# Stage one with two sets of part buffers, turned copies read in source order, and scalings on ScalarE

## What is computed

```python
n = layernorm(x)
q, k, v = split_heads(n @ Wq + bq), split_heads(n @ Wk + bk), split_heads(n @ Wv + bv)
scores = einsum('bhid,bhjd->bhij', q, k)
rel = einsum('bhid,pd->bhip', q, rel_key)
bias = take_along_axis(rel, clip(j - i + p - 1, 0, p - 1), axis=3)
attn = softmax(where(j <= i, (scores + bias) * scale, -inf))
x = x + layernorm(merge_heads(attn @ v) @ Wo + bo)
h = silu(lin(layernorm(x), w1, s1)) * lin(layernorm(x), w2, s2)
h = gelu(lin(h, h1, sh1))
h = gelu(lin(h, h2, sh2))
x = x + layernorm(lin(h, w3, s3))
```

## Time and profile before

| | us |
|---|---|
| median of 3 runs | 740.18 (736.39 to 741.16) |
| the profiled execution | 739.48 |
| its span | 737.4 |
| PE busy | 644.0 (87%) |
| ACT busy | 572.1 (78%) |
| DVE busy | 540.2 (73%) |
| POOL busy | 247.7 (34%) |
| PE on the chain that ended last | 53% |

### The profile page before, as it was taken

The page is one execution under the profiler, slowest core; times in us unless marked ns, Lnnn a source line. Parts: engine busy times, 40 slices in busy tenths (PEclk is TensorE's granted clock), DMA queues, the critical chain, the costliest instruction groups (busy, mean ns, idle before and its releaser), DMA issues.

```text
span 737.4 us, 18944 instructions
## 1 busy us (share of the span) xinstructions
PE 644.0 (87%) x8066; PEld 467.7 (63%) x8066; DVE 540.2 (73%) x923; ACT 572.1 (78%) x660; POOL 247.7 (34%) x175
## 2 busy tenths in 40 slices
PE   4877569999999999999999999978799898998993
PEld 2433336676766766857667667655588687786682
DVE  5894787788687877786878777775677668588546
ACT  2784977988989889889898798786577868677573
POOL 2100180370640913706409128000271441731901
PEclk9988767999999999999999999997999999999997
DMA  7487424152241231521412314050300000000001
GB/s 229 110 224 225 133 63 111 35 132 66 50 114 36 73 94 35 128 70 50 106 46 70 96 34 116 24 166 2 100 1 1 0 1 1 1 29 0 5 25 59
DMA packets 39175, 52.82 MB, mean 72 GB/s; under 512 B 5656, under 2 KB 29640, under 8 KB 36680
## 3 DMA queue, kind: packets, MB, share of 16 engines
q1 hardware_dynamic: 39088, 51.58, 25.6%
HBM read 39.00 MB, written 11.81 MB: 69 GB/s over the span
## 4 chain that ended last, share of the span: by engine, by line
PE 53%; DVE 13%; ACT 12%; issue 5%; POOL 2%; DVEq 0%; ACTq 0%; POOLq 0%
PE p_o L1112 16%; PE p_s L1087 13%; PE p_z L1786 8%; PE p_z L1789 8%; DVE probs L1213 6%; ACT probs L1330 6%; PE p_s L1021 5%; POOL hid_lo L1707 1%; DVE res L1967 1%; ACT hid_hi L1890 1%; ACT o_acc L1339 1%; ACT even_b L1034 1%; ACT odd_b L1034 1%; PE p_o L1124 1%; DVE hid_lo L1991 1%
## 5 line engine op out<-in xcount | busy, mean ns | idle before, releaser
L1087 PE MATMUL p_s<-q_sb,k_sb 96*128 96x128 bf16 (+1 forms) x1600 | 172.1, 250 | 9.9 <-ACT probs L1330 4.7
L1330 ACT ACTIVATE probs<-p_s 128x1024 f32<-128x1024 f32 x160 | 156.7, 1017 | 19.9 <-DVE p_s L1222 10.8
L1112 PE MATMUL p_o<-probs,v_sb 128*32 128x128 f32 (+1 forms) x3200 | 159.9, 331 | 7.5 <-ACT o_acc L1339 4.4
L990 POOL TENSOR_SCALAR_AFFINE_SELECT even_b<-even_b 128x2048 f32<-128x2048 f32 x31 | 75.0, 2420 | 261.3 <-ACT even_b L1034 261.3
L1330 ACT ACTIVATE probs<-probs 128x1024 f32<-128x1024 f32 x128 | 133.5, 1055 | 35.7 <-DVE probs L1213 35.4
L1087 PEld LDWEIGHTS p_s<-q_sb,k_sb 96*128 96x128 bf16 x1600 | 113.8, 100 | 69.5 <-issue 29.5
L1213 DVE TENSOR_TENSOR probs<-p_s,even_b 128x1024 f32<-128x1024 f32 x96 | 114.9, 1219 | 16.6 <-PE p_s L1087 16.6
L1112 PEld LDWEIGHTS p_o<-probs,v_sb 128*32 128x32 f32 x3200 | 84.6, 111 | 41.0 <-issue 14.1
L1786 PE MATMUL p_z<-hid_hi,h_hi 128*128 128x512 f32 x256 | 102.0, 399 | 1.7 <-POOL hid_lo L1707 1.7
L1021 PE MATMUL p_s<-q_rows,rel_w 72*128 72x64 bf16 x2048 | 84.5, 197 | 20.1 <-DVE probs L1213 8.7
L1789 PE MATMUL p_z<-hid_lo,h_hi 128*128 128x512 f32 x256 | 100.9, 394 | 0.0
(11 more groups left out here) (182 smaller groups left out, 844.7 us busy)
## 6 DMA issues: line engine op xcount, KB each, us to landing
k_sb<-k_dram SPq DMA_DIRECT2D x48, 192.0 KB
q_sb<-q_dram SPq DMA_DIRECT2D x16, 576.0 KB
q_rows<-qr_dram SPq DMA_DIRECT2D x42, 192.0 KB
q_dram<-q_parts SPq DMA_DIRECT2D x12, 256.0 KB, 3.1
k_dram<-k_parts SPq DMA_DIRECT2D x12, 256.0 KB, 3.2
qr_dram<-q_turned SPq DMA_DIRECT2D x12, 256.0 KB, 3.4
x_all<-in_L_attn_x_dram SPq DMA_DIRECT2D x4, 512.0 KB, 4.2
every<-in_L_ffn_h_w_dram SPq DMA_DIRECT2D x2, 1024.0 KB, 8.4
```

Of the source, the lines that this page charges most:

```text
L990: nc.gpsimd.affine_select(out=far, in_=near, compare_op=ALU.is_ge, fill=0.0, base=-1 - r, pattern=[[0, QB], [-1, MCH * RCH]], channel_mult ...
L1087: last = nc.tensor.matmul(slot[:, c:c + n * BLK], k_sb[hg][:, h * S + j * BLK:h * S + (j + 1) * BLK], ap(q_sb[hg], at, [[HG * S, KROWS], [ ...
L1112: last = nc.tensor.matmul(p_o[32 * h:32 * h + 32, at:at + blocks * BLK], v_sb[hg][:, j, h * 32:(h + 1) * 32], probs[n % PBUFS][:, h, col * ...
L1330: nc.scalar.activation(to, got, ACT.Exp, scale=SCALE).then_inc(t_exp, 1)
```

## The change

- **Two sets.** `q_parts`, `k_parts` and `q_turned` exist twice, batch b uses set b % 2, and each semaphore of stores exists twice. ScalarE waits, from batch 2 on, for the stores of batch b-2 (`stored`). `m_parts` of batches 0 and 1 lies in `x_all`, over tokens of the same batch that are no longer needed; batches 2 and 3 have one new buffer, `m_late`, and ScalarE waits for the first m store on it before it writes batch 3's. The room comes out of `stored_room`, an unused tile. Waits at the end of stage one and in stage two are adjusted to the sets; before the first copy into `even_b`, ScalarE now waits for the m stores of batches 0 and 1.
- **Turned copies.** The same permutation is walked in the order of the source: reads go through 128 neighbouring columns, writes step over eight columns (16 bytes).
- **Scalings.** For batches 1 to 3 the eight scalings of the layer norm are ScalarE's (`scaled`), with scale and bias as pointers: those of batch 1 behind `root(1)`, those of b+2 behind `m_parts` of batch b. VectorE ends a layer norm with `nmr`.
- **Loads.** SP loads `k_sb` and `q_sb` of the second half in batch 2 instead of batch 1.
- **Bound.** The wait for `own` moves behind the first two products of each batch.

```diff
-STORED_ROOM = 5184
+STORED_ROOM = 576
+    def m_parts(b):
+
+        if b >= 2:
+            return m_late[:, :, :]
+        return x_all[0:H, b * S:(b + 1) * S].bitcast(BF16).rearrange("h (m s) -> h m s", m=MPARTS)
     def turned_view(to, part):
 
-        return to[:, part, :].rearrange("p (r i) -> p r i", i=NB)
+        return to[:, part, :].rearrange("p (r i) -> p i r", i=NB)
+
+    def stored(eng, b, sems):
+
+        for done in sems:
+            eng.wait_ge(done[b % 2], (b // 2 + 1) * (16 * PARTS))
 
     def untouched_view(got, part):
 
-        return got[:, part, :].rearrange("p (i r) -> p r i", i=NB)
+        return got[:, part, :].rearrange("p (i r) -> p i r", i=NB)
...
             if b == 2:
-                sp.wait_ge(s_mst, 16)
+                sp.wait_ge(s_mst[0], 16)
                 for hg in range(2):
                     load_m(0, hg)
             if not first:
                 shift(b - 1)
             if b == 1:
-                for done in (s_qst, s_kst, s_rst):
-                    sp.wait_ge(done, 16 * PARTS)
+                stored(sp, 0, (s_qst, s_kst, s_rst))
                 sp.dma_start(q_rows[:, :], ap(qr_dram, 0, [[DROW, PARTS * HD], [0, PARTS], [1, UH * S]])).then_inc(t_qr[0], 16)
-                for hg in range(2):
-                    load_k(0, hg)
-                    load_q(0, hg)
+            if b in (1, 2):
+                load_k(0, b - 1)
+                load_q(0, b - 1)
...
             dve.wait_ge(s_std, b + 1)
+            if not first:
+                dve.wait_ge(s_xh, b)
             nc.vector.reciprocal(rstd[:, :], std[:, :]).then_inc(s_ln, 1)
             dve.wait_ge(s_ln, b * LNS + 4)
             nc.vector.scalar_tensor_tensor(out=nmr[:, :], in0=mv[:, :, 0], scalar=-1.0, in1=rstd[:, :],
                                            op0=ALU.mult, op1=ALU.mult).then_inc(s_ln, 1)
+            if not first:
+                return
             dve.wait_ge(s_ln, b * LNS + 5)
-            if not first:
-                dve.wait_ge(s_tr, b * 2)
...
+        def scaled(b):
+            act.wait_ge(s_xin, b * 16 + 16)
+            act.wait_ge(s_ln, b * LNS + 5)
+            act.wait_ge(s_tr, b * 2)
+            for t in range(NB):
+                last = nc.scalar.activation(xh[:, t, :], x_all[:, b * S + t * E:b * S + (t + 1) * E], ACT.Identity,
+                                            scale=rstd[:, t:t + 1], bias=nmr[:, t:t + 1])
+            last.then_inc(s_xh, 1)
...
             if first:
                 root(1)
+                scaled(1)
...
             if last_batch:
+                act.wait_ge(s_mst[0], 16 * 2)
                 for c in range(FIRST_BEFORE):
                     copy_act(act, "even", c)
 
-            if not first:
-                act.wait_ge(s_turned, b * PARTS)
-                act.wait_ge(s_qst, b * (16 * PARTS))
-                act.wait_ge(s_kst, b * (16 * PARTS))
-            nc.scalar.activation(q_parts[:, 0, :], qf[:, :], ACT.Identity).then_inc(s_hi, 1)
+            if b >= 2:
+                act.wait_ge(s_turned, (b - 1) * PARTS)
+                stored(act, b - 2, (s_qst, s_kst))
+            nc.scalar.activation(q_parts[b % 2][:, 0, :], qf[:, :], ACT.Identity).then_inc(s_hi, 1)
...
+            if b + 2 < B:
+                scaled(b + 2)
             if not last_batch:
                 turn_query(b, 2)
...
             pe.wait_ge(s_pos, b + 1)
-            pe.wait_ge(s_own, b + 1)
             for j in range(2):
...
+                if j == 0:
+                    pe.wait_ge(s_own, b + 1)
```

More of the change, by code:

```diff
@@ L249, in build @@
     far_keep, near_cap = (sb(n, [128, MCH * RCH], F32, one) for n in ("far_keep", "near_cap"))
+    early_parts = [sb(f"{n}0", [128, PARTS, S], BF16, one) for n in ("q_parts", "k_parts", "q_turned")]
     sb("stored_room", [128, STORED_ROOM], F32, one)
     exp_warm = sb("exp_warm", [128, 1], F32, one)
-    q_parts, k_parts = (sb(n, [128, PARTS, S], BF16, one) for n in ("q_parts", "k_parts"))
-    m_parts = sb("m_parts", [H, MPARTS, S], BF16, one)
-    q_turned = sb("q_turned", [128, PARTS, S], BF16, one)
+    q_late, k_late = (sb(f"{n}1", [128, PARTS, S], BF16, one) for n in ("q_parts", "k_parts"))
+    m_late = sb("m_late", [H, MPARTS, S], BF16, one)
+    turned_late = sb("q_turned1", [128, PARTS, S], BF16, one)
+    q_parts, k_parts, q_turned = zip(early_parts, (q_late, k_late, turned_late))
+    def m_parts(b):
+        if b >= 2:
+            return m_late[:, :, :]
+        return x_all[0:H, b * S:(b + 1) * S].bitcast(BF16).rearrange("h (m s) -> h m s", m=MPARTS)
     pone = ExitStack()
@@ L284, in build @@
     s_turned = sem("s_turned")
-    s_rst = sem("s_rst")
+    s_rst = [sem(f"s_rst{p}") for p in range(2)]
     s_pos = sem("s_pos")
@@ L295, in build @@
     s_wabs, s_wany = sem("s_wabs"), sem("s_wany")
-    s_qst, s_kst, s_mst = sem("s_qst"), sem("s_kst"), sem("s_mst")
+    s_qst, s_kst, s_mst = ([sem(f"{n}{p}") for p in range(2)] for n in ("s_qst", "s_kst", "s_mst"))
     t_q = [sem(f"t_q{p}") for p in range(2)]
@@ L427, in sync_one @@
             turned(B - 1, part)
[L428 to L431, removed]
+        for b in (B - 2, B - 1):
+            stored(sp, b, (s_qst, s_kst, s_rst))
+        for p in range(2):
+            sp.wait_ge(s_mst[p], 16 * 2)
         sp.wait_ge(s_gap, B + 3)
@@ L510, in shift_rest @@
             dve.wait_ge(s_mneg, b * 2 + 2)
-            nc.vector.scalar_tensor_tensor(out=m_parts[:, 1, :], in0=p_tr[0:H, :], scalar=-1.0, in1=m_parts[:, 0, :],
+            nc.vector.scalar_tensor_tensor(out=m_parts(b)[:, 1, :], in0=p_tr[0:H, :], scalar=-1.0, in1=m_parts(b)[:, 0, :],
                                            op0=ALU.mult, op1=ALU.subtract).then_inc(s_mr, 1)
@@ L560, in batch @@
             dve.wait_ge(s_hi, b * 2 + 1)
-            nc.vector.tensor_tensor(q_rest[:, :], qf[:, :], q_parts[:, 0, :], ALU.subtract).then_inc(s_rest, 1)
+            nc.vector.tensor_tensor(q_rest[:, :], qf[:, :], q_parts[b % 2][:, 0, :], ALU.subtract).then_inc(s_rest, 1)
             dve.wait_ge(s_hi, b * 2 + 2)
-            nc.vector.tensor_tensor(k_rest[:, :], kf[:, :], k_parts[:, 0, :], ALU.subtract).then_inc(s_rest, 1)
+            nc.vector.tensor_tensor(k_rest[:, :], kf[:, :], k_parts[b % 2][:, 0, :], ALU.subtract).then_inc(s_rest, 1)
             if not last_batch:
@@ L649, in turn_query @@
             act.wait_ge((s_hi, s_mid, s_low)[part], b * 2 + 1)
-            if b > 0 and part == 0:
-                act.wait_ge(s_rst, 16 * PARTS * b)
-            nc.scalar.activation(turned_view(q_turned, part), untouched_view(q_parts, part),
+            if b >= 2 and part == 0:
+                stored(act, b - 2, (s_rst,))
+            nc.scalar.activation(turned_view(q_turned[b % 2], part), untouched_view(q_parts[b % 2], part),
                                  ACT.Identity).then_inc(s_turned, 1)
@@ L682, in batch @@
             act.wait_ge(s_rest, b * 2 + 1)
-            nc.scalar.activation(q_parts[:, 1, :], q_rest[:, :], ACT.Identity).then_inc(s_mid, 1)
+            nc.scalar.activation(q_parts[b % 2][:, 1, :], q_rest[:, :], ACT.Identity).then_inc(s_mid, 1)
             act.wait_ge(s_rest, b * 2 + 2)
-            nc.scalar.activation(k_parts[:, 1, :], k_rest[:, :], ACT.Identity).then_inc(s_mid, 1)
+            nc.scalar.activation(k_parts[b % 2][:, 1, :], k_rest[:, :], ACT.Identity).then_inc(s_mid, 1)
             if not last_batch:
@@ L690, in batch @@
                 low_bits(b)
-            if not first:
-                act.wait_ge(s_mst, b * 16)
+            if last_batch:
+                act.wait_ge(s_mst[1], 16)
             for j in range(2):
```

21 lines of the change are left out of this document (11 added, 10 removed).

## The result

The change makes the kernel slower: 763.21 us (median of 4 runs, 759.99 to 763.84) against 738.28 us of the kernel before (735.77 to 741.16, the three runs above and a fourth), a ratio of 1.0323, 95% interval 1.0291 to 1.0354. The forecast was 733.6 us with a range up to 737.9.

A forecast was written before the change was run, and what follows sets the result against it. Stage one was taken as bound by ScalarE's 8.9 us store wait before batch 2; following the batches, the first exponential moved from 108.99 to 103.1, so 739.48 - 5.9 = 733.6 us, range 730.2 to 737.9.

The forecast's parts named there:

- the price of the turned copy: ScalarE's turned copies in stage one: 1.05 us each instead of 1.98, 0.93 less, with bounds of 1.05 to 1.98.
- the nearest row: Profile row of even_b's copy, writes jumping every 16 elements, 1013 ns; used to price the turned copy at 1.05 us.
- rival B: Turned copies on ScalarE: scattered 2-byte writes cost more than scattered reads; at 3.2 us each, 748 us; chance 0.04.
- the three last copies: Last turned copies of stage one: end earlier but give nothing, since the first exponential waits for VectorE's low part of k.
- rival A: Turned copies in stage one still cost 1.98 us each, 3.9 us more than forecast, 737.5 us; chance 0.2.
- The removed wait: ScalarE's 8.9 us stop before batch 2 for batch 1's k stores goes; its first part starts 7.9 us earlier.
- slack of batch 1's stores: Before batch 3: stores landed by 72.98 at the latest, needed at about 85, 12 us of slack.
- rival D: Batch 1's stores land after 85, from new queue order or slower DMA; 739 us or so; chance 0.03.
- The scalings: Layer norm scalings moved to ScalarE: eight take 3.1 us, VectorE loses 2.2 per batch; the loop itself gains nothing.
- The walk through the batches: Stage one's times followed batch by batch: qf(3) at 77.5, first exponential at 103.1 instead of 108.99, 5.9 us earlier.
- Rival C: TensorE keeps its full 2.4 GHz clock in project(3), 2.6 us less on batch 2's path, 731.0 us; chance 0.13.
- Stage two and three: After the first exponential: instructions kept, same distance to the end, 628 us.

## Why the prediction was wrong, point by point

- **The failed step is the price of the turned copy.** The sum took 1.05 us, and bounds of 1.05 to 1.98; it takes 4.8. The reason that the text gave was "the nearest row", even_b's copy, "whose writes jump every 16 elements". That row has 4-byte elements, 16 of them in a run. Nothing in it is written alone, and nothing is 2 bytes wide, so it could not bound single 2-byte writes. The text did say that both bounds may be exceeded, and left that to rival B. The measured copies put both differences into numbers: 4-byte elements 16 B apart 2.00, 2-byte ones 4.73. No other step is off by nearly as much; the points below give their errors.
- **Rival B was the case, and its chance was too low.** Its mechanism (scattered 2-byte writes dearer than scattered reads) and its place (ScalarE sets the loop) hold. It put 14 us on a copy going from 1.05 to 3.2, 6.5 us per us. A copy of 1.05 would keep ScalarE for some 0.95 and the measured one keeps it for 4.5, 3.6 more, which gives 733.6 + 23 = 757. The remaining 6 are the three last copies, which the text left at nothing because VectorE's low part covered them: at 4.5 us each they end 6.1 us behind it. The slope was a little low: between the kernels with old and new walk the first exponential moves by 26.1 us, without those 6.1 by 20.0, for 2.6 to 2.7 us more a copy, some 7.5 us per us. Its 0.04 rested on "nothing shows such a price". A missing row was taken as evidence that the price is low, where it was no evidence.
- **The line rule of the Trainium skill (Advanced Engine Details and Errata, SBUF Cachelines) pointed the right way, and gives no size.** The text gave rival A, the rule's case, the price of the old copy, 1.98 us, and 737.5 us, 2.0 under its base of 739.48. The kernel with the old walk, where the copies have that price, measured 736.53, 2.0 under the 738.51 of the kernel before beside it. The runs bear out that sum, not that price for the new walk.
- **The removed wait: right.** Two sets alone end stage one 5.5 us earlier, and no wait of ScalarE for a DMA is left. The slack of batch 1's stores was real: with the loads in the old or the new order the time is the same, so rival D falls.
- **The scalings: right in price, and in effect as far as the loop goes.** Eight took 3.18 us (forecast 3.1), one set ends 24.6 us into the span (forecast 24.05). The text said that in the loop they eat what the cheaper copies give; with copies at 1.98 they cost 3.6 us there. Its reason, that they stand between nmr and kf, is not enough by itself: with the turned copies on GpSimd they stand there too, and the loop is 1.7 us faster for them. That kernel also slows VectorE, so the share of each stays open.
- **The walk through the batches: right once the price is set.** With copies at 1.98 it gave, in the expectation above, a first exponential 1.4 us before the measured 107.81, of which 0.8 is the longer last batch, which the walk did not have. With the sets alone it was 1.8 early, 101.7 against 103.49.
- **Rival C: not seen.** project(3) still gets the lower clock. TensorE's row of its first 3 us, in the changed kernel (busy us, PEclk, DMA share, GB/s):

```profile
83.00:86.00 3.00, 3.00 (x4) 0.50 0.75 163
```

and in the kernel with two sets alone:

```profile
63.50:66.50 3.00, 3.00 (x4) 0.50 0.81 315
```

- **Stage two and three: right.** 628.2 us against 628.4.

## What to carry to other kernels

Reordering a copy moves its cost from the reads to the writes, and the two have different prices: read the element size and the distance of the side that will jump, and where no row has both, keep the upper end open. If a permutation of 2-byte data has to be done by an engine, let the reads jump and write in order. A wait that is removed also covered work around it: price every other part of the change on the schedule without that wait, and then look for the idle places that are left, since a copy of 1.9 us cost nothing once it stood in one. And an engine that is idle is not free help: GpSimd's copies and masks lengthen what VectorE does beside them, so look at what runs on both at the time.

## What the runs showed of the hardware

- 2-byte writes 16 B or more apart take 4.5 to 4.8 us per 1024 columns on ScalarE and on GpSimd, 2.3 to 2.4 on VectorE; reads 256 B apart 1.92, 1.95 and 1.02. VectorE did each of the twelve in 0.4 to 0.65 of ScalarE's time. Turning q on VectorE was not tried.
- ScalarE with two pointer operands and 128 columns: eight in 3.18 us, starts 0.39 apart.
- A VectorE subtraction of 128x1024, usually 1.22 us, took 2.96 beside a copy of GpSimd and 3.35 beside a mask; `own`, usually 1.28, took 3.36 beside a mask.
- Between 40 and 60 us TensorE's granted clock is 0.57 in the kernel after, where it is busy for 7.52 of 20 us and idle for 7.02 us ahead of the transposes; before it was 0.83, with 14.90 us busy. It costs nothing there, since ScalarE sets the pace and is busy for 19.95 of those 20 us.
